# One of four score maxima of an attention step goes through a ScalarE copy, and the first pair of maxima products is issued in two halves

## The reference

```python
Q = _lora_linear(x, Wq, bq, Aq, Bq).reshape(N, S, HEADS, HEAD_DIM)
K = _lora_linear(x, Wk, bk, Ak, Bk).reshape(N, S, HEADS, HEAD_DIM)
V = _lora_linear(x, Wv, bv, Av, Bv).reshape(N, S, HEADS, HEAD_DIM)
energy = jnp.einsum('nqhd,nkhd->nhqk', Q, K) / jnp.sqrt(jnp.float32(HEAD_DIM))
attn = jax.nn.softmax(energy, axis=-1)
out = jnp.einsum('nhqk,nkhd->nqhd', attn, V).reshape(N, S, EMBED)
```

## Time and profile before

| | us |
|---|---|
| median of three runs (1894.64 to 1897.63) | 1895.42 |
| the profiled execution, its own time | 1896.61 |
| its span, first to last instruction | 1894.8 |
| TensorE busy / VectorE busy / ScalarE busy | 1852.1 / 1519.5 / 1256.1 |
| mean granted TensorE clock | 0.991 |

### The profile page before, as it was taken

One profiled execution on the slowest core, in us unless ns is written; L12 is line 12 of the kernel. 1 busy time (PEld: TensorE's weight loads), 2 busy tenths in 40 slices (PEclk: granted clock), 3 DMA queues, 4 the chain that ended last, 5 costly groups with the idle time before them and its releaser, 6 DMA issues.

```text
span 1894.8 us, 34221 instructions
## 1 busy us (share of the span) xinstructions
PE 1852.1 (98%) x13114; PEld 759.7 (40%) x13115; DVE 1519.5 (80%) x2717; ACT 1256.1 (66%) x1441; POOL 349.4 (18%) x435
## 2 busy tenths in 40 slices
PE   8899999999999999999999999999999999999997
PEld 5442222222222222222222222222225755699996
DVE  6678999999999999999999999999953432255553
ACT  5456777777777777777777777777786512245442
POOL 5464202020000000000000200000100067323332
PEclk9998999999999999999999999999999999999998
DMA  6332122221111110111212111111112743422221
GB/s 213 121 114 87 43 75 74 83 86 43 34 57 50 46 43 32 43 53 56 84 43 85 46 49 56 45 64 62 41 56 102 280 143 105 126 75 72 72 70 50
DMA packets 81119, 145.74 MB, mean 77 GB/s; under 512 B 12546, under 2 KB 47362, under 8 KB 80980
## 3 DMA queue, kind: packets, MB, share of 16 engines
q1 hardware_dynamic: 72108, 118.40, 18.5%
q0 software_dynamic: 7936, 24.01, 3.7%
q10 hardware_dynamic: 936, 1.44, 0.2%
HBM read 92.94 MB, written 50.61 MB: 76 GB/s over the span
## 4 chain that ended last, share of the span: by engine, by line
PE 88%; DVE 8%; ACT 2%; DMA 1%; issue 1%; POOL 1%; POOLq 0%; ACTq 0%; DVEq 0%
PE ps L1074 25%; PE ps L1063 20%; PE ps L1040 15%; PE ps L1750 7%; DVE mx L1119 6%; PE ps L1322 6%; PE ps L1773 3%; PE ps L1636 3%; PE ps L650 2%; ACT prob L1154 1%; PE ps L667 1%; PE ps L1350 1%; PE ps L1369 1%; DMA qk_parts<-parts 1%; DVE x_t L478 0%
## 5 line engine op out<-in xcount | busy, mean ns | idle before, releaser
L1119 DVE TENSOR_REDUCE mx<-ps 128x1 f32<-128x512 f32 x2048 | 1273.3, 682 | 39.3 <-PE ps L1040 34.6
L1154 ACT ACTIVATE prob<-ps 128x1024 f32<-128x1024 f32 x1024 | 992.3, 1021 | 280.9 <-PE ps L1063 278.5
L1074 PE MATMUL ps<-prob,vs 128*32 128x512 f32 x4096 | 546.4, 605 | 0.7 <-ACT prob L1154 0.7
L1040 PE MATMUL ps<-k_high,q_high 64*128 64x512 bf16 x2048 | 400.6, 388 | 3.8 <-DVE mx L1119 3.3
L1063 PE MATMUL ps<-q_high,k_high 64*128 64x512 bf16 x2048 | 390.2, 378 | 1.6 <-ACT prob L1154 0.5
L1063 PE MATMUL ps<-q_low,k_low 34*128 34x512 bf16 x2048 | 390.5, 378 | 0.0
L1040 PEld LDWEIGHTS ps<-k_high,q_high 64*128 64x128 bf16 x2048 | 99.1, 92 | 647.3 <-DVE mx L1119 626.0
L1182 POOL CAST mb<-turned_sb 16x128 bf16<-16x128 f32 x32 | 9.0, 280 | 876.8 <-ACT turned_sb L1142 853.6
L1063 PEld LDWEIGHTS ps<-q_low,k_low 34*128 34x128 bf16 x2048 | 100.1, 94 | 117.2 <-issue 0.9
L1063 PEld LDWEIGHTS ps<-q_high,k_high 64*128 64x128 bf16 x2048 | 101.5, 96 | 87.4 <-ACT prob L1154 28.6
L1074 PEld LDWEIGHTS ps<-prob,vs 128*32 128x32 f32 x4096 | 80.6, 108 | 118.8 <-issue 113.4
(11 more groups left out here) (153 smaller groups left out, 1371.7 us busy)
## 6 DMA issues: line engine op xcount, KB each, us to landing
k_high<-qk_parts SPq DMA_DIRECT2D x126, 128.0 KB
qk_parts<-parts SPq DMA_DIRECT2D x32, 384.0 KB, 3.0
k_low<-qk_parts SPq DMA_DIRECT2D x128, 64.0 KB
head_out<-head_out_sb SPq DMA_DIRECT2D x32, 256.0 KB, 10.8
q_high<-qk_parts SPq DMA_DIRECT2D x126, 64.0 KB
sorted_in<-zero_row POOLq DMA_DIRECT2D x13, 390.0 KB, 7.2
xs<-sorted_in SPq DMA_DIRECT2D x39, 130.0 KB
q_low<-qk_parts SPq DMA_DIRECT2D x64, 64.0 KB
```

What stands on the lines that cost most here:

```text
L1040: pe.matmul(ps[:, ring.bank((n, m, u)), :], q_high[p][mine, t * P:(t + 1) * P], k_high[p][mine, c * CH:(c + 1) * CH], start=True, stop=Tru ...
L1074: mm = pe.matmul(ps[32 * j:32 * j + 32, 7, :], vs[buf(h)][:, kt, :], prob[:, kt % 2, j * CH:(j + 1) * CH], start=(kt == 0), stop=(kt == KT ...
L1119: dve.tensor_reduce(mx[n % 2][:, at, c:c + 1], ps[:, ring.bank(what), :], AX.X, ALU.max).then_inc(s_ring, 1)
L1154: act.activation(prob[:, kt % 2, :].rearrange("p (u c n) -> p u c n", u=2, c=2)[:, :, half, :], ps[:, 2 * half:2 * half + 2, :], ACT.Exp). ...
```

## The change

In each of the 490 steps the unit u = 0 of the second pair is no longer read by VectorE from PSUM. ScalarE copies it to one of two SBUF buffers `unit_sb`, and VectorE takes the maximum of that copy later, behind the two reductions of the next step's first pair. The bank is free when ScalarE has copied. The first pair is issued in two halves, u = 0 ahead of `scores(this, 1)` and u = 1 behind it, and each half waits for its own place. `scores` takes its row halves in the order 1, 0 for half 0 and 0, 1 for half 1 (it was 0, 1 for both). The buffers lie where wgT will lie, so wgT is loaded after attention. The wait of GpSimd for the transposed maxima counts the copies too.

```diff
+def carried(n, m, u):
+    return u == 0 and m % 2 == 1 and (n >= 2 or n == 1 and m >= LEAD)
...
-                    self.add((n, m, u), "dve", count)
+                    self.add((n, m, u), "act" if carried(n, m, u) else "dve", count)
...
+        unit_sb = buffers("unit_sb", [P, CH], F32, Region(nc, wg_at, wg_at + NCOPY * 4 * CH), NCOPY)
...
-            for dst, name in ((wgT, "wgT"), (wuT, "wuT"), (wdT, "wdT")):
+            for dst, name in ((wuT, "wuT"), (wdT, "wdT")):
...
+        def max_half(pe, h, m, u):
+            if m == 0 and u == 0:
+                stacked(pe, h)
+            wait_for_places(pe, (num(h), m, u))
+            max_product(pe, h, m, u)
...
-                    for u in range(2):
+                    for u in (1 - i, i):
...
+                    if beside:
+                        max_half(pe, who, first, 0)
                     scores(*this, 1)
                     if beside:
-                        max_pair(pe, who, first)
+                        max_half(pe, who, first, 1)
...
+        def reduce_carried(dve, n, m):
+            if m < 0:
+                n, m = n - 1, PAIRS - 1
+            if not carried(n, m, 0):
+                return
+            dve.wait_ge(s_turned, ring.taken((n, m, 0)))
+            dve.tensor_reduce(mx[n % 2][:, m // CPB, m % CPB:m % CPB + 1],
+                              unit_sb[carried_before(n, m) % NCOPY][:], AX.X, ALU.max).then_inc(s_carried, 1)
...
                     reduce_pair(dve, (0, n), m)
+                    if m % 2 == 0:
+                        reduce_carried(dve, n, m - 1)
...
+        def carry(act, g):
...
+            what, k = (who, first + 1, 0), carried_before(who, first + 1)
+            act.wait_ge(s_max, ring.made(what))
+            wait(act, s_carried, k - NCOPY + 1)
+            act.copy(unit_sb[k % NCOPY][:], ps[:, ring.bank(what), :]).then_inc(s_turned, 1)
...
                 for kt in range(KT):
+                    carry(act, KT * n + kt)
                     exps(n, kt)
...
+            sp.wait_ge(s_carried, carried_before(NH - 1, PAIRS))
+            sp.dma_start(wgT[:], io["wgT"]).then_inc(s_shared, 16)
             store_x1(0)
```

More of the change, by code:

```diff
@@ L69 @@
 SLOTS = 6
+NCOPY = 2
 BESIDE = 8
@@ L87, in wait, with carried_before @@
         eng.wait_ge(semaphore, n)
+def carried(n, m, u):
+    return u == 0 and m % 2 == 1 and (n >= 2 or n == 1 and m >= LEAD)
+def carried_before(n, m):
+    return sum(carried(k, j, 0) for k in range(n + 1) for j in range(PAIRS if k < n else m))
 class Region:
@@ L191, in block_kernel @@
         colffn = held("colffn", [P, B, 2, HALF])
+        wg_at = held.at
         wgT = held("wgT", [P, HALF, F])
@@ L370, in block_kernel @@
         s_turned = sem("s_turned")
+        s_carried = sem("s_carried")
         s_mb = sem("s_mb")
@@ L1028, in wait_for_places, with max_product, stacked @@
                 wait(pe, semaphore, max([n for e, n in before if e == engine], default=0))
+        def max_product(pe, h, m, u):
+            p, n, t, c = buf(h), num(h), m // CPB, m % CPB
+            mine = slice(u * HROWS, (u + 1) * HROWS)
+            pe.matmul(ps[:, ring.bank((n, m, u)), :], q_high[p][mine, t * P:(t + 1) * P],
+                      k_high[p][mine, c * CH:(c + 1) * CH], start=True, stop=True).then_inc(s_max, 1)
+        def stacked(pe, h):
+            p = buf(h)
+            pe.wait_ge(s_stack[p], STACK * (nth(h) + 1) - (STACK // 2 if p == 0 else 0))
+            if num(h) == 0:
+                pe.wait_ge(s_stack_first, STACK // 2)
         def max_pair(pe, h, m):
-            p, n, t, c = buf(h), num(h), m // CPB, m % CPB
             if m == 0:
[L1034 to L1037, removed]
+                stacked(pe, h)
+            wait_for_places(pe, (num(h), m, 0), (num(h), m, 1))
             for u in range(2):
-                mine = slice(u * HROWS, (u + 1) * HROWS)
-                pe.matmul(ps[:, ring.bank((n, m, u)), :], q_high[p][mine, t * P:(t + 1) * P],
-                          k_high[p][mine, c * CH:(c + 1) * CH], start=True, stop=True).then_inc(s_max, 1)
+                max_product(pe, h, m, u)
+        def max_half(pe, h, m, u):
+            if m == 0 and u == 0:
+                stacked(pe, h)
+            wait_for_places(pe, (num(h), m, u))
+            max_product(pe, h, m, u)
         def turn_maxima(pe, h):
@@ L1117, in reduce_pair @@
                 at = u * HT + t
+                if carried(*what):
+                    continue
                 dve.wait_ge(s_max, ring.made(what))
@@ L1120, in reduce_pair @@
                                   ALU.max).then_inc(s_ring, 1)
+        def reduce_carried(dve, n, m):
[6 more added lines that the diff above has]
+                              unit_sb[carried_before(n, m) % NCOPY][:], AX.X, ALU.max).then_inc(s_carried, 1)
         def negate(dve, n):
             dve.wait_ge(s_ring, ring.taken((n, PAIRS - 1, 1)))
+            wait(dve, s_carried, carried_before(n, PAIRS))
             dve.tensor_reduce(mneg[:], mx[n % 2][:], AX.X, ALU.max, negate=True).then_inc(s_neg, 1)
@@ L1134, in attend_vector @@
                         invert(dve, int(n == NEXT_AT + 3), m // 4, m // 4 + 1)
+            reduce_carried(dve, NH - 1, PAIRS - 1)
             negate(dve, NH - 1)
+        def carry(act, g):
+            n, kt = (g - 2) // KT, (g - 2) % KT + 1
+            first, who = LEAD + 2 * (kt - 1), n + 1
+            if first >= PAIRS:
+                first, who = first - PAIRS, n + 2
+            if g < 2 or who >= NH:
+                return
+            what, k = (who, first + 1, 0), carried_before(who, first + 1)
+            act.wait_ge(s_max, ring.made(what))
+            wait(act, s_carried, k - NCOPY + 1)
+            act.copy(unit_sb[k % NCOPY][:], ps[:, ring.bank(what), :]).then_inc(s_turned, 1)
         def take_turned(act, n):
@@ L1179, in split_maxima @@
             p = n % NB
-            pool.wait_ge(s_turned, n + 1)
+            pool.wait_ge(s_turned, ring.taken((n, "turned")))
             pool.wait_ge(s_mrows[p], 64 + MROWS * (n // NB))
```

## The result

The changed kernel takes 1862.91 us (median, 1862.1 to 1865.23) against 1895.03 (1891.87 to 1897.63) for the kernel before, run beside it. The ratio is 0.983, with a 95% interval from 0.981 to 0.985. The forecast was 1866: faster, by 32 us instead of 29. The profiled execution has a span of 1861.2 us and a granted clock of 0.991, as before.

A forecast was written before the change was run, and what follows sets the result against it. A loop through VectorE and TensorE was taken to set the 2.49 us step. 1896.61 - 34 (steps) - 8 (transposes) + 12 (sums copies) + 1 was given as 1867; with that execution 1.2 above the median, 1866 us, range 1854 to 1966.

The forecast's parts named there:

- The loop through VectorE and TensorE set 2.49, and the copy shortens it: Attention step: replacing VectorE's maximum by ScalarE's copy in the loop takes 2.49 us to 2.42, gaining 490 x 0.07 = 34 us.
- The copy starts when VectorE would, 0.43 behind the pair: ScalarE's copy in each step: starts 0.43 us after the second pair's issue, with 0.49 as upper bound.
- case B: Rival on ScalarE's copies: they start 0.10 after the product, step 2.46, 1886 us; chance 0.11.
- TensorE's own work is the floor, VectorE just under it: Attention step: TensorE's own work and turns need 2.42 us; VectorE's four maxima need 2.39, 0.03 under the step.
- ScalarE has room: ScalarE in each step: idles 0.55 us; with the copy it needs 2.33, under 2.42.
- Case C: Rival on ScalarE: its full loop, 2.53 at worst, eats the gain in about half the steps, 1890 to 1900; chance 0.09.
- The sums copy costs 30 x 0.39 = 12 us: Once a head: ScalarE's copy of the head's sums delays the unit's copy, losing 12 us, or 0 if slack takes it.
- The transposes give 30 x 0.27 = 8 us: Steps with a transpose: the earlier first half gets VectorE's maximum done in time, saving a 0.27 wait, 8 us gained.
- Maxima from SBUF cost as much as from PSUM, 0.60: VectorE's maximum of a copied unit, 512 columns: 0.60 us from SBUF, as from PSUM; 0.05 dearer would cost 10 us.
- The split is free because row halves overtake: TensorE's matmuls in a step: those on a free row half start ahead, so five slots of 0.22 remain, cost 0.
- wgT's later load is hidden: Load of wgT after attention: lands some 5.4 us after issue, with 27 us of cover; costs 0, at most 1 us.

The follow-up runs named there:

- experiment 6: The changed kernel with VectorE's maximum of a copied unit taken over only 64 of its 512 columns: 1858.7 us, ratio 0.9797.
- experiment 8: The changed kernel with each unit copied by ScalarE in two instructions of 256 columns: 1877.55 us, ratio 0.9898.
- Experiment 4: The changed kernel with unit 0 of the pair in the step of the sums copy (m = 11) left to VectorE: 1854.34 us, ratio 0.9784.
- experiment 3: The kernel before with only the first pair cut into two halves, no copy by ScalarE: 1894.43 us, ratio 0.9995.
- experiment 1: The kernel before with the scores' matmuls listed by row half (0, 0, 1, 1) instead of alternating: 1896.41 us, ratio 1.0002.
- experiment 2: The changed kernel with the first pair issued whole behind the scores again, with one common wait, copy kept: 1901.55 us, ratio 1.0034.

## Why the prediction was right

Its steps, one by one:

- **The loop through VectorE and TensorE set 2.49, and the copy shortens it.** Right: a plain step fell from 2.489 to 2.407. I forecast 0.07 a step and 490 x 0.07 = 34 us; it is 0.082, and 40 us. Why it came out 0.01 larger than the 0.07 of waiting: weighting starts 0.30 behind the last maxima matmul (883.48 - 883.18) instead of 0.32. What makes that turn shorter I didn't test.
- **The copy starts when VectorE would, 0.43 behind the pair** (882.50 - 882.07), not 0.49. Right; case B falls. Right too that it takes 0.59 and is seen 0.05 later.
- **TensorE's own work is the floor, VectorE just under it.** Right: experiment 6 freed VectorE and the step didn't move, and by experiment 8 the copy's end has 0.03 to spare. That it is TensorE's work follows by leaving out the other two; no experiment made that work itself shorter.
- **ScalarE has room.** Right, but it is thinner than the page makes clear: 298.67 of 300 us is counted, with records that overlap. Case C (1890 to 1900) falls: copy to exponential 0.50, exponentials 0.92 apart, and 0.98 from the second exponential to the next copy, which starts as soon as its product is done.
- **The sums copy costs 30 x 0.39 = 12 us.** Right: that step takes 2.80, 0.39 over a plain one. Experiment 4 takes 0.28 of it back.
- **The transposes give 30 x 0.27 = 8 us.** Too large, and the reason was wrong. I credited the earlier first half, but by experiment 3 the split alone leaves the transpose step at 3.00. And I took the maximum that the transpose waits for to be done in time. It isn't; VectorE's rows ahead of the transpose in the changed kernel's timeline:

```profile
459.92 0.68 DVE L1169 TENSOR_REDUCE mx<-unit_sb 128x1 f32<-128x512 f32 x1
460.70 0.22 DVE L1176 TENSOR_REDUCE mneg<-mx 128x16 f32<-128x64 f32 x1
460.84 0.68 DVE L1158 TENSOR_REDUCE mx<-ps 128x1 f32<-128x512 f32 x1
...
461.57 0.09 PEld L1080 LDWEIGHTS ps<-ident,mneg 128*16 128x16 f32 x1 [0.38 <-DVE mx L1158]
```

  The product of m = 1 is issued at 460.04 and done at 460.43, but VectorE has a copied unit (to 460.60) and the fold (from 460.70) to do first, so its maximum ends at 460.84 + 0.68 = 461.52. Over a plain step a transpose now costs 2.734 - 2.407 = 0.33 instead of 0.48: 30 x 0.155 = 5 us.
- **Not foreseen:** the first step of a new head's maxima took 0.09 more than a plain one before (2.58) and takes no more now: 30 x 0.09 = 3 us.
- **Maxima from SBUF cost as much as from PSUM, 0.60.** Right: 675 ns against 683, the next start 0.59 behind against 0.60 to 0.61. The Trainium skill, "VectorE: DVE Perf Modes", section on the TRN2 errata, gives SBUF sources 58 cycles of overhead and PSUM 120, from which I estimated SBUF 0.065 cheaper. That isn't seen here: 0.01 is.
- **The split is free because row halves overtake.** Right, by the timeline after and by experiment 1. The Trainium skill, "TensorE: Matmul & The Clock Gate", Part 3 on packing small matmuls, has matmuls in strict order; for matmuls on different row halves these runs don't agree. By it, experiment 1 should have been far slower; it took 1896.41 us against 1895.61.
- **wgT's later load is hidden.** Right, though the load is slower than assumed. Three views of the changed kernel: SyncE's timeline; the DMA issues with KB and us to landing; and TensorE's line of the first user, with min/median/max ns and first and last start:

```profile
1423.77 0.51 SPq L1360 DMA_DIRECT2D wgT<-in_wgT  x1
```

```profile
wgT<-in_wgT SPq DMA_DIRECT2D x1, 512.0 KB, 10.8
```

```profile
L1394 PE MATMUL ps<-h2T,wgT x128: 592/592/676, 1457.0 to 1614.2; 128*128 x96, 128*128 128x512 f32 x32
```

  It lands 10.8 us after issue instead of 5.4, at 1434.6, and is first used at 1457.0: 22 us of cover are left.

The sum as measured: -40 for the plain steps, -5 for the transposes, -3 for the first steps of a head, +12 for the sums copies, that is -36; the spans differ by 1894.8 - 1861.2 = 33.6. From the first weighting to the last it is -34.7, so a good 1 us of the estimate isn't placed. A few single steps of 2.9 to 3.3, with waits of other kinds, differ between the two traces by about that. The remaining 1 lies outside attention.

That the forecast came out 3 us off is in part luck: 6 us too little in the plain steps and 3 us not foreseen at the first steps of a head stand against 3 us too much at the transposes and the 1 us that isn't placed. The recorded sum is also added up a little short: 1896.61 - 34 - 8 + 12 + 1 is 1867.6, not 1867.

What the prediction did not see is a second reason why the copy needs the split. It credited the split with the transposes alone. But the pair whole waits once for two engines, and with the pair whole and its one common wait kept, the kernel would have been 0.3% slower (experiment 2).

## What to carry to other kernels

When two engines come to free the places that one instruction group waits for, give each instruction the wait for its own place: here one wait for two engines in front of a pair cost 0.067 us in most steps and kept the copy from gaining anything. A stall in a loop between two engines can be taken away by an engine with idle time, but look for the steps in which that engine has something else ahead; leaving those to the old path was worth 8.6 us here. Read which engine bounds a step by freeing it in an experiment: three engines over 99% busy and a chain of 41% through VectorE told less than one kernel that took most of a maximum away from it.

## What the runs showed that I had not expected

- A wait for two engines' semaphores ahead of a TensorE pair: 0.12 us from the release to the weight load and 0.15 to the matmul, where a wait for one is seen in the weight load after 0.05 (experiment 2 and the changed kernel). The second wait is an instruction of its own, 0.051 us, and the profile lists the idle time as "issue".
- Matmuls on a free half of the rows start ahead of earlier ones in the list, ahead of up to one matmul of the other half, at no cost (experiment 1, and the timeline after).
- Two copies of 256 columns from PSUM by ScalarE follow each other 0.26 apart and end 0.64 after the start, against 0.59 for one of 512 (experiment 8): splitting costs 0.06.
- The same 512 KB load took 10.8 us to land at the end of attention and 5.4 at its start; what it shared the queue with I didn't test.
